# A four-layer language-model tower: decay attention with its scores copied to SBUF one step ahead, and without its overwritten bf16 matmuls

## What is computed

```python
scores = jnp.einsum('bhqd,bhkd->bhqk', q, k) / jnp.sqrt(jnp.float32(dk))
mask = jnp.tril(jnp.ones((s, s), bool))
p_ = jax.nn.softmax(jnp.where(mask, scores, -1e+32), axis=-1) * mask
distcum = jnp.cumsum(p_, axis=-1)
disttotal = p_.sum(-1, keepdims=True)
dist = jax.lax.stop_gradient(jnp.sqrt(jnp.clip((disttotal - distcum) * pos, 0.0)))
total_effect = jnp.clip(jnp.exp(dist * gamma), 1e-05, 100000.0)
scores = jnp.where(mask, scores * total_effect, -1e+32)
p = jax.nn.softmax(scores, axis=-1)
out = jnp.einsum('bhqk,bhkd->bhqd', p, v)
```

## Time and profile before

| what | value |
|---|---|
| time, median of 3 runs | 3239.71 us (3229.29 to 3274.91) |
| the profiled execution's own time | 3245.55 us |
| its span, first to last instruction | 3243.8 us |
| busy: PE, DVE, ACT, POOL | 2771.9, 1960.9, 1513.2, 1261.0 us |
| mean granted clock of TensorE | 0.848 of full |
| first instructions of the steps 0 and 127 of the stage on DVE | 1824.7 and 3020.7 us |

### The profile page before, as it was taken

How to read it: one execution, slowest core, us unless ns; L and a number is a source line. 1 busy time by engine, 2 the same in 40 slices (tenths; PEclk the granted TensorE clock), 3 DMA queues, 4 the chain that set the end, 5 groups by cost and what they waited for, 6 DMA issues and landing times. The chain is left out here.

```text
span 3243.8 us, 60046 instructions
## 1 busy us (share of the span) xinstructions
PE 2771.9 (85%) x21812; PEld 1904.3 (59%) x21812; DVE 1960.9 (60%) x3888; ACT 1513.2 (47%) x2961; POOL 1261.0 (39%) x1551
## 2 busy tenths in 40 slices
PE   7998699992999999999997687888888888888476
PEld 6887477772555555555554465565555555555365
DVE  4995477775444454444444567666776677676624
ACT  1442366663333332233222366666666666666442
POOL 5661244443100000000000366655665666565371
PEclk9996699995999999999998568767887787686587
DMA  1110000000000000000000000000000000000002
GB/s 42 39 41 4 7 2 2 2 2 24 1 1 0 0 0 0 0 0 0 0 0 21 1 1 2 1 1 1 2 1 1 1 2 1 1 2 1 4 1 53
DMA packets 31576, 21.60 MB, mean 7 GB/s; under 512 B 24553, under 2 KB 28649, under 8 KB 31364
## 3 DMA queue, kind: packets, MB, share of 16 engines
q0 software_dynamic: 6144, 9.84, 1.3%
q1 hardware_dynamic: 25220, 8.94, 1.2%
HBM read 14.58 MB, written 4.19 MB: 6 GB/s over the span
## 5 line engine op out<-in xcount | busy, mean ns | idle before, releaser
L1245 DVE TENSOR_TENSOR prod<-c_h,act 128x512 f32<-128x512 f32 x352 | 243.4, 692 | 481.0 <-PE c_h L1097 439.0
L1177 ACT ACTIVATE act<-c_h 128x512 f32<-128x512 f32 x352 | 210.2, 597 | 655.9 <-PE c_h L1097 655.9
L1428 POOL TENSOR_TENSOR d_decay<-d_later,d_posg 128x768 f32<-128x768 f32 x128 | 232.6, 1817 | 437.5 <-DVE d_later L1827 437.5
L1124 PE MATMUL c_out<-e_w,hid 128*128 128x64 f32 x2816 | 388.7, 281 | 0.1
L1124 PEld LDWEIGHTS c_out<-e_w,hid 128*128 128x128 f32 x2816 | 340.6, 191 | 79.5 <-issue 79.3
L1071 POOL TENSOR_TENSOR x_rest<-flatT,x_hm 64x512 f32<-64x512 bf16 (+1 forms) x33 | 38.2, 1156 | 748.8 <-ACT x_hm L1157 724.8
L1469 PE MATMUL d_T<-ident,d_p 128*128 128x128 f32 x768 | 165.7, 336 | 184.2 <-ACT d_pT L1603 104.5
L1827 DVE TENSOR_TENSOR_SCAN d_later<-d_cont,d_ex 128x768 f32<-128x768 f32 x128 | 225.1, 1759 | 73.8 <-ACT d_ex L1621 73.8
L1097 PE MATMUL c_h<-x_hm,e_w_hh 128*128 128x512 bf16 x704 | 267.5, 380 | 0.9 <-ACT wT L1170 0.9
L1097 PE MATMUL c_h<-x_hm,e_w_mm 128*128 128x512 bf16 x704 | 267.6, 380 | 0.0
L1097 PE MATMUL c_h<-x_hl,e_w_lh 128*128 128x512 bf16 x704 | 267.4, 380 | 0.0
(11 more groups left out here) (356 smaller groups left out, 6287.5 us busy)
## 6 DMA issues: line engine op xcount, KB each, us to landing
out_h<-g_Y SPq DMA_DIRECT2D x8, 512.0 KB, 4.0
rows<-in_table,idx POOLq DMA_INDIRECT x128
e_w<-in_e_w SPq DMA_DIRECT2D x2, 704.0 KB
d_cont<-in_d_cont SPq DMA_DIRECT2D x1, 384.0 KB
e_w<-in_e_w SPq DMA_DIRECT2D x1, 352.0 KB
d_conv<-in_d_conv SPq DMA_DIRECT2D x1, 320.0 KB
d_wqk<-in_d_wqk SPq DMA_DIRECT2D x1, 256.0 KB
d_pos<-in_d_pos SPq DMA_DIRECT2D x1, 192.0 KB
```

What stands on the lines that cost most here:

```text
L1124: last = nc.tensor.matmul(bo[:, b * D:(b + 1) * D], hid[u][:, b * P:(b + 1) * P], w2[:, c, :], start=(c == 0 and b == 0), stop=(c == NCH - ...
L1177: nc.scalar.activation(act1[u][:], b1[u][:], ACT.Silu).then_inc(S["activated"], 1)
L1245: nc.vector.tensor_tensor(prod[u][:], b3[u][:], act1[u][:], ALU.mult).then_inc(S["multiplied"], 1)
L1428: pool.tensor_tensor(decay[u][:], later[u][:, 0:2 * SEG].rearrange("p (e s) -> p e s", e=2), posg[:, h:h + 2, :], ALU.mult).then_inc(U["pl ...
```

## The change

- A ring of four SBUF tiles `kept` [128, 2, 384] f32 holds the scores. ACT copies them there from PSUM (new signal `S_kept`), in its pass K for step K+1, behind the second copy of the transposed p.
- PE issues `scores(K+1)` in its pass K, and may overwrite the PSUM buffer once the copy of step K-1 is made; before, it waited for `weighed`.
- DVE takes the maxima, the two subtractions and `weighed` from `kept` in place of PSUM. `weighed` and its maxima move from behind the scan (step K-1) to ahead of it, for step K-2.
- POOL: "placed" moves to the start of the next pass, for K-1; "shifted2" to the end of the pass, behind the group work.
- ACT: the first copy of the transposed p and the exponential of the scores come first; the last Exp of decay comes behind the new copy; the exponential of p2 comes last in the pass.
- The four bf16 matmuls of each step, their tile and its memset are gone.

```diff
@@ -1272,8 +1272,7 @@
-    KEEP_V, KEEP_P, KEEP_T = 3, 3, 8
-    WARM = 4
+    KEEP_V, KEEP_S, KEEP_P, KEEP_T = 3, 4, 3, 8
...
-        ident_b, fill = m_.sb("d_ident_b", [P, P], BF16), m_.sb("d_fill", [P, 512], BF16)
+        ident_b = m_.sb("d_ident_b", [P, P], BF16)
...
+        kept = [m_.sb(f"d_kept{u}", [P, 2, SEG]) for u in range(KEEP_S)]
...
@@ -1374,17 +1374,17 @@ (gpsimd)
                     if step_there(K - 1):
                         u = (K - 1) % 2
+                        h = 2 * ((K - 1) % PAIRS)
+                        pool.wait_ge(U["scanned"], K)
+                        if K - 1 >= 2:
+                            pool.wait_ge(U["weighed"], K - 2)
+                        pool.tensor_tensor(decay[u][:], later[u][:, 0:2 * SEG].rearrange("p (e s) -> p e s", e=2),
+                                           posg[:, h:h + 2, :], ALU.mult).then_inc(U["placed"], 1)
                         pool.wait_ge(U["inv_total"], 2 * K)
                         pool.wait_ge(U["placed"], K)
...
-                    if step_there(K - 2):
-                        u, w = (K - 2) % 2, (K - 2) % KEEP_P
-                        pool.wait_ge(U["max2_made"], 2 * (K - 1))
-                        pool.tensor_tensor(long(p2[w]), long(p2[w]), wide(mx2[u], 1, P), ALU.subtract)
-                        pool.tensor_tensor(short(p2[w]), short(p2[w]), wide(mx2[u], 0, HALF), ALU.subtract)\
-                            .then_inc(U["shifted2"], 1)
                     if j == 0:
...
-                    if step_there(K):
-                        u = K % 2
-                        h = 2 * j
-                        pool.wait_ge(U["scanned"], K + 1)
...
+                    if step_there(K - 2):
+                        u, w = K % 2, (K - 2) % KEEP_P
+                        pool.wait_ge(U["max2_made"], 2 * (K - 1))
+                        pool.tensor_tensor(long(p2[w]), long(p2[w]), wide(mx2[u], 1, P), ALU.subtract)
+                        pool.tensor_tensor(short(p2[w]), short(p2[w]), wide(mx2[u], 0, HALF), ALU.subtract)\
+                            .then_inc(U["shifted2"], 1)
@@ -1445,7 +1443,7 @@ (tensor, scores)
                     if K >= 2:
-                        pe.wait_ge(U["weighed"], K - 1)
+                        pe.wait_ge(U["S_kept"], K - 1)
@@ -1514,12 +1512,8 @@ (tensor, loop)
-                    if step_there(K):
-                        scores(K)
-                        if quad_there((K - 6) // 2):
-                            pe.wait_ge(Q["attT_kept"], (K - 6) // 2 + 1)
-                        for _ in range(WARM):
-                            nc.tensor.matmul(bO[:], ident_b[:], fill[:], start=True, stop=True)
+                    if step_there(K + 1):
+                        scores(K + 1)
                     if step_there(K - 3):
                         turn(K - 3, 0)
@@ -1610,25 +1604,17 @@ (scalar, loop)
+                    if step_there(K - 3):
+                        keep_turned(K - 3, 0)
+                    if step_there(K):
+                        act.wait_ge(U["shifted"], 2 * (K + 1))
+                        nc.scalar.activation(ex[K % 2][:], ex[K % 2][:], ACT.Exp).then_inc(U["exped"], 1)
                     if step_there(K - 1):
                         u = (K - 1) % 2
                         act.wait_ge(U["scaled"], K)
                         nc.scalar.activation(decay[u][:], decay[u][:], ACT.Ln, bias=1e-18).then_inc(U["log_done"], 1)
                         act.wait_ge(U["log_done"], K)
                         nc.scalar.activation(decay[u][:], decay[u][:], ACT.Exp, scale=0.5).then_inc(U["root_done"], 1)
-                    if step_there(K):
...
@@ -1651,6 +1637,16 @@ (scalar, loop)
                     if step_there(K - 3):
                         keep_turned(K - 3, 1)
+                    if step_there(K + 1):
+                        act.wait_ge(U["scored"], K + 2)
+                        if K + 1 >= KEEP_S:
+                            act.wait_ge(U["weighed"], K + 2 - KEEP_S)
+                        nc.scalar.activation(kept[(K + 1) % KEEP_S][:], bS[(K + 1) % 2][:, :, 0:SEG], ACT.Copy)\
+                            .then_inc(U["S_kept"], 1)
+                    if step_there(K - 1):
+                        u = (K - 1) % 2
+                        act.wait_ge(U["root_done"], K)
+                        nc.scalar.activation(decay[u][:], decay[u][:], ACT.Exp, scale=-1.0).then_inc(U["decay_made"], 1)
...
@@ -1703,6 +1699,10 @@ (scalar, end of the step)
+                    if step_there(K - 2):
+                        w = (K - 2) % KEEP_P
+                        act.wait_ge(U["shifted2"], K - 1)
+                        nc.scalar.activation(p2[w][:], p2[w][:], ACT.Exp).then_inc(U["exped2"], 1)
@@ -1764,7 +1764,6 @@ (vector)
-                nc.vector.memset(fill[:], 1.0).then_inc(ready, 1)
...
@@ -1782,18 +1781,16 @@ (vector, loop)
-                        dve.wait_ge(U["scored"], K + 1)
-                        if K >= 2:
-                            dve.wait_ge(U["exped"], K - 1)
-                        nc.vector.tensor_reduce(mx[u][:, 1], long(bS[u]), AX, ALU.max).then_inc(U["max_made"], 1)
...
+                        dve.wait_ge(U["S_kept"], K + 1)
+                        nc.vector.tensor_reduce(mx[u][:, 1], long(kept[K % KEEP_S]), AX, ALU.max).then_inc(U["max_made"], 1)
...
-                        nc.vector.tensor_tensor(long(ex[u]), long(bS[u]), wide(mx[u], 1, P), ALU.subtract)\
+                        nc.vector.tensor_tensor(long(ex[u]), long(kept[K % KEEP_S]), wide(mx[u], 1, P), ALU.subtract)\
                             .then_inc(U["shifted"], 1)
...
@@ -1819,6 +1816,18 @@ (vector, ahead of the scan)
+                    if step_there(K - 2):
+                        u, w = K % 2, (K - 2) % KEEP_P
+                        dve.wait_ge(U["decay_made"], K - 1)
...
+                        nc.vector.scalar_tensor_tensor(p2[w][:], decay[u][:], 1e-5, kept[(K - 2) % KEEP_S][:],
+                                                       ALU.max, ALU.mult).then_inc(U["weighed"], 1)
...
@@ -1833,18 +1842,6 @@ (vector, behind the scan)
-                    if step_there(K - 1):
-                        u, w = (K - 1) % 2, (K - 1) % KEEP_P
-                        dve.wait_ge(U["decay_made"], K)
...
-                        nc.vector.scalar_tensor_tensor(p2[w][:], decay[u][:], 1e-5, bS[u][:, :, 0:SEG],
-                                                       ALU.max, ALU.mult).then_inc(U["weighed"], 1)
...
```

More of the change, by code:

```diff
@@ L1320, in phase_decay_attention @@
         U = {name: m_.sem(f"d_{name}") for name in
-             ("scored", "max_made", "shifted", "exped", "scanned", "inv_total", "placed", "scaled", "log_done",
+             ("scored", "S_kept", "max_made", "shifted", "exped", "scanned", "inv_total", "placed", "scaled", "log_done",
               "root_done", "decay_made", "weighed", "max2_made", "shifted2", "exped2", "turned", "pT_kept")}
@@ L1331, in phase_decay_attention @@
         LOADS = 18
-        READY = 15
+        READY = 14
         FIRST, LAST = -16, NQ + 8
@@ L1618, in _ @@
                         nc.scalar.activation(decay[u][:], decay[u][:], ACT.Exp, scale=0.5).then_inc(U["root_done"], 1)
-                    if step_there(K):
-                        act.wait_ge(U["shifted"], 2 * (K + 1))
-                        nc.scalar.activation(ex[K % 2][:], ex[K % 2][:], ACT.Exp).then_inc(U["exped"], 1)
-                    if step_there(K - 1):
[L1623 to L1631, removed]
                     if j == 0:
@@ L1784, in _ @@
                         u = K % 2
[L1785 to L1789 removed]
+                        dve.wait_ge(U["S_kept"], K + 1)
+                        nc.vector.tensor_reduce(mx[u][:, 1], long(kept[K % KEEP_S]), AX, ALU.max).then_inc(U["max_made"], 1)
+                        nc.vector.tensor_reduce(mx[u][:, 0], short(kept[K % KEEP_S]), AX, ALU.max).then_inc(U["max_made"], 1)
                         dve.wait_ge(U["max_made"], 2 * K + 1)
@@ L1792, in _ @@
                             dve.wait_ge(U["scanned"], K - 1)
-                        nc.vector.tensor_tensor(long(ex[u]), long(bS[u]), wide(mx[u], 1, P), ALU.subtract)\
+                        nc.vector.tensor_tensor(long(ex[u]), long(kept[K % KEEP_S]), wide(mx[u], 1, P), ALU.subtract)\
                             .then_inc(U["shifted"], 1)
                         dve.wait_ge(U["max_made"], 2 * K + 2)
-                        nc.vector.tensor_tensor(short(ex[u]), short(bS[u]), wide(mx[u], 0, HALF), ALU.subtract)\
+                        nc.vector.tensor_tensor(short(ex[u]), short(kept[K % KEEP_S]), wide(mx[u], 0, HALF), ALU.subtract)\
                             .then_inc(U["shifted"], 1)
@@ L1821, in _ @@
                             nc.vector.tensor_reduce(ss2[:], sq2[:], AX, ALU.add).then_inc(G["spread2"], 1)
+                    if step_there(K - 2):
+                        u, w = K % 2, (K - 2) % KEEP_P
+                        dve.wait_ge(U["decay_made"], K - 1)
```

(21 more changed lines are left out.)

3 lines of the change are left out of this document (removed).

## The result

The changed kernel takes 3292.03 us (median, 3284.78 to 3308.38) against 3234.5 us for the kernel before (3225.95 to 3274.91) in the same comparison: ratio 1.0194, 95% interval 1.0134 to 1.0254. The profiled execution took 3285.48 us, 39.9 more than that of before.

What follows compares the result with a forecast made beforehand. No engine is full; DVE's queue and PE's scores take turns, 9.42 us a step. Exclusion and a slower clock outweigh the gain: (9.55 - 9.42) x 128 = +17 us, 3263 profiled, 3257 median; range 3110 to 3345, likeliest case 3200 to 3304.

Steps and rivals of the forecast that it cites:

- the exclusion: DVE instructions with two SBUF inputs and POOL's block each other, holding what they share 7.8 to 9.6 us a step.
- the scores a step ahead: Issuing scores early removes DVE's 1.76 us wait and hides 0.57 us of exponential; alone 7.1 us a step.
- ACT's queue comes next: After the score wait goes, ACT's late copy `S_kept`, 0.8 us, holds up DVE's next step, all on the path.
- The two layouts at the fast clock: Step timings at the fast clock: 8.97 us a step with exclusion, 7.55 with exclusion hidden in slack.
- The layout: Forecast step timings with exclusion and part of the slow clock's cost: 38.2 us a group, 9.55 a step.
- the four pairs: The steps j = 0 to 3 of a group, forecast at 12.3, 7.8, 9.2 and 8.9 us.
- the clock in j = 0: Step j = 0 taken halfway at 12.3 us, between 10.3 at the fast clock and 14.3 at 1.2 GHz.
- the slow layout: Step timings at 1.2 GHz all through: j = 0 14.3 us, j = 2 9.2, 10.05 a step.
- The upper bound of 111: Most the four bf16 matmuls could cost if all on the path: 0.87 us a step, 111 us; 0 taken.
- The second rival: Slower: without bf16 blocks TensorE stays at 1.2 GHz for most of the stage, 3321 to 3353 us; chance 0.31.
- the point: The forecast median time of the whole changed kernel, 3257 us.

Runs made afterwards that it cites:

- the first experiment: The kernel before without its four bf16 matmuls a step, nothing else changed: 3334.22 us, ratio 1.0269.
- the fastest kernel: The changed kernel with maxima and both subtractions from PSUM and the four bf16 matmuls put back: 3081.77 us, ratio 0.9490.

## Why the prediction was right, and where it was off

**The outcome.** The forecast was little change, leaning to slower, for a reason that could be read in the trace: the exclusion takes back what the scores a step ahead give. That holds. With the subtractions out of it the change would have gained 3.2% (ratio 0.9678), and 5.1% with the bf16 matmuls in place too (0.9490). With it and with the matmuls the change gains nothing (1.0034). The loss of 1.9% that was measured is then almost all the matmuls' removal.

**The scores a step ahead.** DVE's wait for the scores and for the exponential went, and the copy's 0.8 us was right. That ACT's queue comes next was half right: DVE waits only 0.5 us a step for the copy.

**The exclusion.** Forecast were maxima of 1.5 to 2.5 us for the long subtraction and `weighed`, measured 2.30 and 1.79 (medians 1.84 and 1.30). "Shifted2" was forecast at 2.5 us and more, measured 2.42 in the median and 2.49 at most. y was forecast at 4.3 us, measured 4.61 in the step shown. The two layouts at the fast clock put the exclusion at 8.97 - 7.55 = 1.42 us a step; by the stages of the runs the subtractions' share of it is 1.00 (without the matmuls) and 1.24 (with them). The layout gave 12.3, 7.8, 9.2 and 8.9 us for the four pairs, 38.2 together, and the steps 8 to 123 took 13.68, 6.97, 9.80 and 8.66, 39.1.

**The term that was mis-sized is the clock in j = 0.** I took this step halfway between 10.3 (2.4 GHz) and 14.3 us (1.2 GHz), because in the earlier trace rows the clock came back within the convolution. The runs showed 13.3 and 14.3 us in turn. With 3.3 or 4.0 us of idle PE ahead, the transposes and the projection of q run at 1.2 GHz in both (0.87 and 1.22 us, against 0.52 and 0.70 at the fast clock). In the one kind of step the convolution does so from end to end (4.38 us, the 14.3 of the slow layout); in the other the clock comes back within it (3.30 us), and that saves only this 1.1 us, not 2. The mean of 13.68 is 1.38 us above the term, 1.38 x 32 = 44 us; j = 2 adds 0.6 x 32 = 19, j = 1 gives back 27 and j = 3 gives back 8. That the sum came out so near is thus in part these opposite errors. Behind it stands a reading that was right only in part. The bf16 matmuls have no place on the path, but the first experiment prices them at 88 us. The upper bound of 111 was for all of them standing on the path, and at the fast clock; line L1522 has 167.6 us busy in the trace of before, 1.31 a step, so as a bound it was low. PE's waits at the transposes said that their time was free, not that their effect was. That the slow clock costs less outside j = 0 holds in the new order (j = 0 to 3 change by +0.86, +0.10, +0.32 and -0.28 us when the matmuls go), but not in the order of before, where j = 1 and j = 3 lose as much as j = 0. The second rival, the clock, is thus true as a mechanism, though the clock of the stage, 0.63, stayed above the 0.6 from which this rival was to decide, and its times, 3321 and more, weren't reached. The Trainium skill, page "TensorE: Matmul & The Clock Gate", section "Part 4: PE-mode transpose", says that transposes in PE's transpose mode don't count as busy PE in the same way, and that the full clock doesn't come with them. No run here separates the transposes' share.

**The rest.** The stage lost 29 us where 17 were forecast. The last layer's 12.9 us more in the profiled execution was in no term, and is scatter by the other runs. The 35 us between the point and the median are thus 12 of the stage, 11 of the untouched layers (12.9 behind it, less 2.3 ahead) and 12 from how the profiled execution lies: I put it 6 us above the median of the runs, and it lay 6.5 below.

## What to carry to other kernels

Before an operand moves from PSUM to SBUF, count the DVE instructions that get a second SBUF input by it, and look at what POOL does at those moments: where two subtractions read was worth 153 us here (127 of them in the stage), about all that the scores a step ahead gave. A copy that frees a PSUM buffer need not be what everybody reads: let early readers stay on PSUM, and give the copy to the late one. Matmuls whose result is overwritten can stand in slack and still carry the clock; measure them by taking them out alone, and don't remove them together with another change.

## What the runs showed that was not expected

- Who pays for the exclusion depends on the order, and on a start that comes 0.1 us earlier or later. In the order of before, with SBUF inputs, the long subtraction kept a median of 682 ns and `weighed` went to 2510; in the new order it is 1840 and 1304.
- Taking four hidden matmuls (1.3 us of PE) out of each step of the kernel before lowered the clock of the stage from 0.74 to 0.63 and cost 88 us; doubling them in the fastest kernel raised it from 0.86 to 0.89 and cost 56 us.
- An untouched layer behind the stage took between 223.0 and 240.8 us in the profiled executions of these kernels, and the untouched layers ahead of it differed by up to 37 us, beside a difference of 39.9 between the two kernels.
